# TensorE's program for the layer stack, written out step by step instead of as a loop over pairs of steps in each layer

## The reference, cut to what matters

```python
x = x + attn(layernorm(x))                      # 16 heads of 8, causal
y = layernorm(x)
for i in range(6):
    y = attn_layer(shift_tokens(y), Wqkv[i], q_scale[i], k_scale[i], Wo[i]) + y
    y = ffn_layer(shift_tokens(y), ln_g[i], ln_b[i], W1[i], b1[i], W2[i], b2[i]) + y
x = x + y
# attn_layer: 16 heads of 64; q and k l2-normalised, scaled, rotated; each window of 32
#   queries sees its own 32 keys and the 32 before; softmax; values; @ Wo
# ffn_layer: layernorm, @ W1, a * gelu(gate), @ W2
```

## Time and profile before

| | |
|---|---|
| time, median of 3 runs | 3477.61 us (3473.73 to 3481.7) |
| profiled execution, its own time | 3467.71 us |
| its span, first to last instruction | 3465.9 us |
| mean granted clock of TensorE | 0.979 |
| TensorE busy, share of the span | 93% |
| VectorE, ScalarE, GpSimd busy | 84%, 81%, 77% |
| chain that ended last | PE 75%, issue 10%, DVE 6%, POOL 5% |

### The profile page before, as it was taken

The page is one execution under the profiler, slowest core; times in us unless marked ns, Lnnn a source line. Parts: engine busy times, 40 slices in busy tenths (PEclk is TensorE's granted clock), DMA queues, the critical chain, the costliest instruction groups (busy, mean ns, idle before and its releaser), DMA issues.

```text
span 3465.9 us, 129619 instructions
## 1 busy us (share of the span) xinstructions
PE 3224.8 (93%) x51488; PEld 2289.5 (66%) x51488; DVE 2896.2 (84%) x5656; ACT 2801.5 (81%) x5313; POOL 2685.9 (77%) x1798
## 2 busy tenths in 40 slices
PE   8999799899999899998999999999999999998996
PEld 5777466666666666675667766666766677766665
DVE  6999788788888888897779898888988788887784
ACT  5777588778888788887889888888988788887884
POOL 1001598778888889998789998889988889988883
PEclk9999899999999999999999999999999999999998
DMA  2000011111211111211112211112211112211111
GB/s 66 0 0 0 7 34 37 37 29 39 59 38 39 39 28 51 57 39 35 31 34 53 50 38 38 39 34 55 50 35 39 39 31 54 51 39 33 33 39 51
DMA packets 127341, 129.59 MB, mean 37 GB/s; under 512 B 62380, under 2 KB 75824, under 8 KB 126832
## 3 DMA queue, kind: packets, MB, share of 16 engines
q1 hardware_dynamic: 123232, 112.38, 13.3%
q10 hardware_dynamic: 3600, 9.50, 0.9%
HBM read 19.04 MB, written 2.10 MB: 6 GB/s over the span
## 4 chain that ended last, share of the span: by engine, by line
PE 75%; issue 10%; DVE 6%; POOL 5%; SPq 1%; DMA 1%; ACT 1%; DVEq 0%; POOLq 0%; ACTq 0%
PE ps L1313 23%; PE ps L1335 9%; PE ps L1328 8%; PE ps L1344 7%; PE ps L1357 7%; PE ps L1305 6%; PE ps L1367 4%; PE ps L1169 3%; POOL area L446 2%; PE ps L1161 2%; POOL AQb L453 2%; PE ps L1158 2%; DVE area L991 2%; PE ps L1181 1%; PE ps L1154 1%
## 5 line engine op out<-in xcount | busy, mean ns | idle before, releaser
L1313 PE MATMUL ps<-Wqkv,xsT 128*128 128x512 f32 x2304 | 1138.3, 617 | 9.0 <-DMA Wqkv<-ffn_Wqkv 3.4
L446 POOL TENSOR_TENSOR area<-area,tab 128x512 f32<-128x512 f32 x768 | 960.6, 1280 | 108.8 <-ACT area L634 107.7
L1313 PEld LDWEIGHTS ps<-Wqkv,xsT 128*128 128x128 f32 x2304 | 403.9, 196 | 341.1 <-issue 240.3
L468 POOL TENSOR_TENSOR area<-area,lsum 128x1024 f32<-128x1024 f32 x192 | 365.7, 1905 | 284.9 <-DVE lsum L932 284.8
L453 POOL TENSOR_TENSOR area<-area 128x1024 f32<-128x1024 f32 x192 | 452.8, 2374 | 46.8 <-DVE area L991 46.8
L634 ACT ACTIVATE area<-ps 128x512 f32<-128x512 f32 x768 | 455.1, 593 | 35.2 <-PE ps L1313 34.4
L453 POOL TENSOR_TENSOR AQb<-AQb,area 128x1024 f32<-128x1024 f32 x192 | 449.5, 2364 | 0.1
L639 ACT ACTIVATE area<-area 128x1024 f32<-128x1024 f32 x384 | 396.5, 1065 | 0.1
L1335 PE MATMUL ps<-Wo,area 128*128 128x128 f32 x3072 | 376.4, 281 | 20.9 <-issue 20.8
L1335 PEld LDWEIGHTS ps<-Wo,area 128*128 128x128 f32 x3072 | 356.4, 194 | 33.8 <-issue 25.4
L1328 PEld LDWEIGHTS ps<-BD,area 64*64 64x64 f32 x12288 | 270.0, 133 | 144.8 <-issue 133.4
(11 more groups left out here) (124 smaller groups left out, 6416.3 us busy)
## 6 DMA issues: line engine op xcount, KB each, us to landing
BD<-area SPq DMA_DIRECT2D x1440, 64.0 KB, 2.0
Wqkv<-ffn_Wqkv ACTq DMA_DIRECT2D x12, 512.0 KB, 3.9
x2s<-x2s SPq DMA_DIRECT2D x96, 56.0 KB, 2.1
Wo<-ffn_Wo SPq DMA_DIRECT2D x6, 512.0 KB, 4.9
Wqkv<-ffn_Wqkv ACTq DMA_DIRECT2D x12, 256.0 KB, 3.1
W<-ffn_W SPq DMA_DIRECT2D x6, 341.0 KB
x2s<-x2s SPq DMA_DIRECT2D x96, 7.5 KB, 2.5
x2s<-x2s SPq DMA_DIRECT2D x96, 0.2 KB, 1.9
```

Source lines behind the costliest of these rows:

```text
L446: pool.tensor_tensor(b4[:, :, here], q4[:, :, there], s4[:, :, here], ALU.mult).then_inc((s_bq, s_bk)[j], 1)
L468: pool.tensor_tensor(p3, p3, lsum[:, 1, :].unsqueeze(2).broadcast_to([P, HEADS, 2 * WIN]), ALU.mult).then_inc(s_pn, 1)
L1313: mm(home(kind + part), xsT[:, par, t * P:(t + 1) * P], Wqkv[:, w0:w0 + 512], start=True, stop=True).then_inc(done, 1)
```

## The change

TensorE, and it alone, no longer goes through `stack_steps`. A new function, `stack_steps_straight`, calls its `step` for n = 0 to 98 with plain integers, so all 99 steps stand in its instruction stream one after another. The work, its order and the counts that the semaphores reach are as before; the waits that exist only for integer step numbers now stand in every step. VectorE, ScalarE, GpSimd and SyncE keep their loops. `live` is moved out so that both functions can use it.

```diff
+        def live(n):
+            return [0 <= n - lag < UNITS for lag in range(4)]
+
         def stack_steps(eng, step, lags):
-
-            def live(n):
-                return [0 <= n - lag < UNITS for lag in range(4)]
...
+        def stack_steps_straight(step, lags):
+
+            for n in range(UNITS + lags):
+                u = n % SEQS
+                step(n, u, u % 2, live(n), n // SEQS)
...
-            stack_steps(pe, step, 3)
+            stack_steps_straight(step, 3)
```

## The result

The changed kernel takes 3344.95 us in the median of four runs (3330.92 to 3348.17), the kernel before 3479.65 us beside it: a ratio of 0.9603, 95% interval 0.9572 to 0.9633. Its profiled execution took 3348.17 us, 119.5 less than the 3467.71 of before. The forecast was 3360 for the median, and -116 us on the profiled execution.

A forecast was written before the change was run, and what follows sets the result against it. TensorE was taken to bound the kernel; -87 - 5 - 47 + 5 + 15 + 3 = -116 us on the profiled 3467.7 gave 3352, and with the median 10 us above it 3361, rounded to 3360; range 3302 to 3425.

The forecast's parts named there:

- (b): TensorE's register operations in 60 loop steps: they go, -5 us.
- (d): TensorE's clock: of 60 us lost to falls, eight falls of 1.6 us stay, 13 us, so -47 us.
- (e): TensorE's waits for block-diagonal copies ahead of `values`: 41 exposed steps at 0.65 us, 26 us against 21, +5 us.
- (g): Wqkv's arrival at each layer's second step: 3.4 us stays, fetch packets behind the weight loads add 3 us.
- (a): TensorE's loop back edges: their gaps ahead of each step's first work go, wholly on the path, -87 us.
- (f): TensorE's instruction fetch: stalls where 256-instruction packet boundaries fall in the scores, 78 us against 63, +15 us.
- (c): Waits formerly only in integer-numbered steps, now in all of TensorE's steps: they end before TensorE arrives, 0 us.
- unseen places: Packet boundaries 46 to 157 instructions into a step, modulo 256: stall fades until 78, rises from 85 to 1.5 us at 127.
- (1): Other engines' loops become the bound, each loop step waiting about 1.07 us for the copies: 3405 us, chance 0.14.
- (2): Instruction fetch costs nothing in TensorE's straight code: 3299 us, chance 0.08.
- (3): Wandering packet boundary stalls TensorE's scores in most steps and the clock falls too: slower, 3517 us, chance 0.05.
- (4): Each straight packet of TensorE costs what the branch did: time within noise, 3478 us, chance 0.04.

The follow-up runs named there:

- twopass: Changed kernel with TensorE partly looping again, two passes of four steps in each layer, six taken back edges in all; 3382.09 us, ratio 0.9721.
- pin230: Changed kernel plus 72 semaphore increments ending step 0 and 1 to 3 ending each step from 3, packet boundary fixed at 230; 3470.39 us, ratio 0.9984.
- pin230_mid: pin230 with the 1 to 3 increments of each step moved from its end to just ahead of its first scores; 3269.74 us, ratio 0.941.
- all: Changed kernel with the stacks of VectorE, ScalarE, GpSimd and SyncE written out too; 3336.89 us, ratio 0.9598.
- mid_all: pin230_mid with the stacks of VectorE, ScalarE, GpSimd and SyncE written out too; 3258.82 us, ratio 0.9364.
- start230: Changed kernel with 72 semaphore increments at the end of step 0 and none later, so the packet boundary wanders on from 230; one run, 3346.85 us.
- pin100: Changed kernel plus 202 semaphore increments ending step 0 and 1 to 3 ending each step from 3, packet boundary fixed at 100; 3379.09 us, ratio 0.9724.

## Why the prediction was right, point by point

The time was right to 15 us and the sum on the profiled execution to 4, but that is better than its terms. The gain of (b) and (d) together was 18 us too large, (e) was 14 us too dear and of the wrong sign, (g) was 3 us for nothing; they cancel, and that is luck. The largest term, (a), and the size of (f) were right.

(a) Back edges, -87: right, -87.0; the group ahead of L1288 is gone, and TensorE has no branch left. twopass put six back at 3.2 us each.

(b) Register operations, -5, and (d) clock, -47: together TensorE's busy time in the 92 steps fell by 33.8 us (2734.99 to 2701.18), not by 52. The step that failed is the sum over before's falls. In before 24 steps are under 0.985, 18 at 0.94 to 0.96 and six at 0.90 or 0.91, and their busy time is 44 us over that of the others, not 60. At the prediction's own 1.6 us for each fall, 24 of them are 38 us; the 60 was what was left of 65 after a small allowance. The rest of it is spread over clean steps, and the written-out form has it as well (clean steps of both kernels have the same busy time to 0.05 us, so (b) was next to nothing). After the change six steps are at 0.95 (37, 39, 42, 80, 83, 89), 10 us; 13 were forecast. 44 - 10 = 34, the measured difference.

(c) Extra static waits, 0: right; step 67 has all of them and takes 29.00 us.

(e) Waits ahead of `values`, forecast 26 us, measured 10.1, from 19 in the same steps: -9 instead of +5. The failed step is the 41 exposed steps at 0.65 us. There are 19 such waits, at 0.5 us: six for H, one for a copy, and 12 for ScalarE's area, which the term did not have. Nor are they in steps 4 to 14 of a layer alone: three are in its steps 2 and 15 (steps 47, 50 and 66). The loop step of the earlier trace rows with its 1.07 us was a bad sample for a TensorE without loops; why the copies are on time now was not tried. Part of the 19 us went with the back edges: twopass, with six of them, has 9 us more of these waits.

(f) Fetch, forecast 78 us, measured 76 ahead of L1363, L1341, L1311, L1334 and L1350; +13 against +15. By zones (without L1334): steps 3 to 13 9.5 forecast, 7.4 measured; 17 to 31 11 and 13.1; 32 to 51 32 and 25.6; 52 to 60 4 and 0; 61 to 79 0 and 0; 80 to 94 22 and 24.0; steps 14 to 16, for which I had no figure, have 3.0. The stalls return at step 80; I said 82. The place moved by 3 instructions a step as worked out: in steps 3 to 7 the stall comes after 302, 304, 307, 310, 313 instructions. The unseen places were not as drawn: from 69 to 124 a stall of 0.5 to 1.2 us is there at once and stays flat (one, in step 18, is 2.1), where I had it fade, and rise again from 85 to 1.5 at 127.

That this term came out is owed to the change leaving nothing at the steps' ends. The reason that it rests on, that the place alone sets the price, is wrong, as pin230 and pin230_mid show with 3470 and 3270 us at the same place, and as step 49 of before showed. The prices came from straight code of the same make, and so held in straight code of that make.

(g) Wqkv, +3: 0. 3.3 us where there were 3.4.

With these: -87 - 34 - 9 + 13 = -117; the 92 steps lost 119.6. The other 2 to 3 us are gaps of under 0.15 us each, which have no rows.

The rivals. (1) gave the other engines' loops 71 us; the waits are 10, and writing out the other engines takes off most of them (10.1 to 3.6 us in `all`, 6.3 to 1.9 in mid_all). (2), free fetch, did not happen here, but pin230_mid is that case: 10 us of stalls, and a time of 3270. The Trainium skill's rule (Runtime: NRT & Kernel Launch, section Instruction fetch mechanics), that crossing a 16 KiB boundary is mostly hidden, does not describe the changed kernel (76 us) and does describe pin230_mid. (3) was built as well: pin230 has a stall in 91 of the 92 steps and 24 falls of the clock, 31.57 us a step, 2.57 over 29.0, and it is level with before; the 2.6 us from which that rival was said to decide was the right number, its price of 3.3 us a step was too high. (4) is out by the ratio.

## What to carry to other kernels

Writing out TensorE's loop took about 5 us off the path for each taken branch, 3 of them the gap at the branch itself (3.1 us in the change, 3.2 in twopass); the other four engines, whose branches take 40 to 67 ns, brought 8 to 15 us together. What is given back is fetch: look for "issue" idle time in the middle of the densest runs of small instructions, at a place that moves by the same few instructions each step, and count from step to step before blaming the data. If it is there, pad the steps to a whole number of packets and try where the padding stands, not only how much of it: the same one to three idle instructions a step cost 125 us against the changed kernel at the step's end (pin230) and gained 75 ahead of the scores (pin230_mid).

## What the runs showed of the hardware

- The packet ahead of the first scores' boundary started 0.3 us before the step in pin230_mid and 7.5 us into it, 0.6 us into the scores, in pin230. Every stall of over 0.5 us in steps 3 to 94 of the kernels here ended 2.1 to 3.2 us after the start of the last packet before it. That this packet holds the missing instructions is read from these times; the trace does not name them.
- When a packet starts is not set by the boundary's place alone; where the sequencer has something of its own to do matters too. The exact rule is open: pin230 against start230, and step 4 of pin230 against its step 3, show the effect of 1 to 3 increments at the step's end, pin230_mid shows that it goes away a quarter of a step later, and no run says why.
- Sequencer increments, 51 ns each on the record, take 0.15 us each in a row (34.3 us for 236 and 9.0 for 72, with TensorE idle).
- Stalls of 0.4 to 1.8 us in all 92 steps (pin100, 0.8 us in the mean) left the granted clock at 1.00 in every step; with stalls of 1.5 to 2.5 us (pin230) it was at about 0.95 in 24 steps, with 1.7 us more of busy time each.
